# Router logits with the router as stationary operand, and a mixture softmax held on 32 partitions

## What is computed

```python
router_probs = softmax(einsum('bsh,he->bse', x, w_router))
gate_weights = softmax(einsum('bsh,he->bse', x, w_gating) / GATE_TEMP)   # GATE_TEMP = 0.1
g = einsum('bsh,ehf->ebsf', x, w_gate)
u = einsum('bsh,ehf->ebsf', x, w_up)
h = silu(g) * u
expert_out = einsum('ebsf,efh->ebsh', h, w_down)
cw = router_probs * gate_weights
cw = cw / (sum(cw, axis=-1) + 1e-09)
out = einsum('ebsh,bse->bsh', expert_out, cw)
```

## Time and profile before

| | |
|---|---|
| median of 3 runs | 1153.64 us (1153.35 to 1153.64) |
| the profiled execution | 1153.37 us, of which the span from first to last instruction is 1151.4 us |
| granted TensorE clock | 0.999 of full speed |
| busy share of the span | PE 98%, DVE 79%, ACT 61%, POOL 54% |

### The profile page before, as it was taken

How to read it: one execution, slowest core, us unless ns; L and a number is a source line. 1 busy time by engine, 2 the same in 40 slices (tenths; PEclk the granted TensorE clock), 3 DMA queues, 4 the chain that set the end, 5 groups by cost and what they waited for, 6 DMA issues and landing times.

```text
span 1151.4 us, 16819 instructions
## 1 busy us (share of the span) xinstructions
PE 1133.6 (98%) x5102; PEld 928.9 (81%) x5102; DVE 915.2 (79%) x2002; ACT 703.7 (61%) x1370; POOL 622.4 (54%) x480
## 2 busy tenths in 40 slices
PE   8999999999999999999999999999999999999997
PEld 4777888888888888888888888888888888888885
DVE  6798877878888788877878778788887888778765
ACT  6675565655656565575655666566565655756564
POOL 1386564654556455464655556455464655556453
PEclk9999999999999999999999999999999999999999
DMA  4240212102021110212102021111212102020110
GB/s 129 69 128 1 75 37 65 46 20 65 28 74 38 47 43 23 74 37 66 46 12 73 28 75 37 47 38 28 74 38 66 46 6 78 28 72 30 47 51 15
DMA packets 82713, 57.61 MB, mean 50 GB/s; under 512 B 35360, under 2 KB 64192, under 8 KB 82624
## 3 DMA queue, kind: packets, MB, share of 16 engines
q1 hardware_dynamic: 82624, 56.54, 16.8%
HBM read 48.13 MB, written 8.39 MB: 49 GB/s over the span
## 4 chain that ended last, share of the span: by engine, by line
PE 96%; DVE 1%; ACT 1%; DMA 0%; issue 0%; POOL 0%; SPq 0%; POOLq 0%; DVEq 0%; ACTq 0%
PE g L280 10%; PE u L280 10%; PE u L282 10%; PE g L282 10%; PE u L281 10%; PE g L281 10%; PE y L280 10%; PE y L282 10%; PE y L281 10%; PE n_ps L287 2%; PE m_ps L280 1%; PE m_ps L282 1%; PE m_ps L281 1%; PE m_ps L372 1%; PE m_ps L371 1%
## 5 line engine op out<-in xcount | busy, mean ns | idle before, releaser
L1125 POOL TENSOR_TENSOR hid_lo<-hid,hid_hi 128x512 fp32r<-128x512 f32 x255 | 341.3, 1338 | 416.7 <-ACT hid_hi L574 416.5
L568 ACT ACTIVATE gate<-g 128x512 f32<-128x512 f32 x512 | 305.5, 597 | 326.7 <-PE g L282 325.1
L848 DVE TENSOR_TENSOR hid<-gate,u 128x512 f32<-128x512 f32 x512 | 348.5, 683 | 165.1 <-ACT gate L568 133.9
L574 ACT ACTIVATE hid_hi<-hid 128x512 fp32r<-128x512 f32 x512 | 321.1, 627 | 38.5 <-DVE hid L848 38.0
L854 DVE TENSOR_TENSOR hid_lo<-hid,hid_hi 128x512 fp32r<-128x512 f32 x257 | 210.7, 820 | 1.8
L280 PE MATMUL g<-xe_hi,w_hi 128*128 128x512 f32 x512 | 206.4, 403 | 0.1
L280 PE MATMUL u<-xe_hi,w_hi 128*128 128x512 f32 x512 | 199.9, 390 | 1.7 <-DVE hid L848 1.7
L280 PE MATMUL y<-hid_hi,w_hi 128*128 128x512 f32 x512 | 200.1, 391 | 0.3 <-ACT hid_hi L574 0.2
L282 PE MATMUL y<-hid_hi,w_lo 128*128 128x512 f32 x512 | 199.8, 390 | 0.0
L282 PE MATMUL g<-xe_hi,w_lo 128*128 128x512 f32 x512 | 199.7, 390 | 0.0
L281 PE MATMUL g<-xe_lo,w_hi 128*128 128x512 f32 x512 | 199.6, 390 | 0.0
(11 more groups left out here) (205 smaller groups left out, 1131.7 us busy)
## 6 DMA issues: line engine op xcount, KB each, us to landing
cw_b<-cw_scratch SPq DMA_DIRECT2D x128, 256.0 KB, 3.3
x_sb<-x_in SPq DMA_DIRECT2D x16, 256.0 KB, 3.1
out_scratch<-acc_t SPq DMA_DIRECT2D x60, 64.0 KB, 2.3
ffn<-out_scratch SPq DMA_DIRECT2D x15, 256.0 KB, 2.7
x_out<-o_sb SPq DMA_DIRECT2D x15, 256.0 KB, 2.2
stage<-wgate_in SPq DMA_DIRECT2D x8, 256.0 KB, 2.9
stage<-wup_in SPq DMA_DIRECT2D x8, 256.0 KB, 3.4
stage<-wdown_in SPq DMA_DIRECT2D x8, 256.0 KB, 4.2
```

What stands on the lines that cost most here:

```text
L568: nc.scalar.activation(gate[:, k % 2, :], g_ps[k % 2][:], ACT.Silu).then_inc(gate_ready, 1)
L574: nc.scalar.activation(hid_hi[:, k % RING, :], hid[:, k % RING, :], ACT.Copy).then_inc(hi_ready, 1)
L848: nc.vector.tensor_tensor(hid[:, k % RING, :], gate[:, k % 2, :], u_ps[k % 2][:], ALU.mult).then_inc(hid_ready, 1)
L1125: nc.gpsimd.tensor_tensor(hid_lo[:, k % RING, :], hid[:, k % RING, :], hid_hi[:, k % RING, :].bitcast(f32), ALU.subtract).then_inc(lo_pool, 1)
```

## The change

The router becomes the stationary operand. Two products with 512 streamed tokens replace eight short ones: `router` (128 x 32) by `xe_hi`, then the high router (128 x 16) by `xe_lo`. The logits now come out with 32 rows (high and low logits) on the partitions and tokens on the free axis. VectorE turns them with one 32x32-block transposition of [32, 512], after which each of 32 partitions holds 16 tokens of 32 values; all softmax tiles are [32 partitions, 16 tokens, 2, 8]. The weights are written into columns 0 to 7 of blocks of 32 columns of `v_sb`, and a second transposition of [32, 512] gives `cw_t` with one expert per partition, 512 tokens in a row. TensorE's `turn_cw` and ScalarE's copy `cw_t` are gone, and two waits with them. The factor 10 of the second softmax is multiplied into the router once, at the start, instead of into the logits of every chunk. ScalarE's `silus` stands at k = 29 instead of 28.

```diff
-TENSOR_AT = {"turn_cw": 4, "turn_x": 5, ...
+TENSOR_AT = {"turn_x": 5, ...
-SCALAR_AT = {"cw_t": 3, "hi_x": 8, ... "silus": 28}
+SCALAR_AT = {"hi_x": 8, ... "silus": 29}
...
-        lg, e_neg, e_pos = (sb(n, [P, NT, 2, E]) for n in ("lg", "e_neg", "e_pos"))
...
+        lg, e_neg, e_pos = (sb(n, [SMALL, SEQ // SMALL, 2, E]) for n in ("lg", "e_neg", "e_pos"))
...
             def mix_turn_x(c):
                 pe.wait_ge(xn_ready, 2 * c + 1)
-                pe.wait_ge(cw_t_ready, c)
...
-                for j in range(NT):
-                    t, at = slice(j * P, (j + 1) * P), 4 * E * j
-                    nc.tensor.matmul(m_ps[:, at:at + 4 * E], xe_hi[:, par, t], router[:], start=True, stop=False)
-                    last = nc.tensor.matmul(m_ps[:, at:at + 2 * E], xe_lo[:, par, t], router[:, 0, :], start=False, stop=True)
-                last.then_inc(logits_ready, 1)
-
-            def mix_turn_cw(c):
-                pe.wait_ge(cw_ready, c + 1)
-                nc.tensor.transpose(n_ps[:, 0:P], cw_pad[:], ident[:]).then_inc(cw_turned, 1)
+                nc.tensor.matmul(m_ps[0:4 * E, :], router[:].rearrange("p h q -> p (h q)"), xe_hi[:, par, :], start=True, stop=False)
+                nc.tensor.matmul(m_ps[0:2 * E, :], router[:, 0, :], xe_lo[:, par, :], start=False,
+                                 stop=True).then_inc(logits_ready, 1)
...
-            def mix_cw_t(c, first):
-                act.wait_ge(cw_turned, c + 1)
-                if not first:
-                    act.wait_ge(cw_stored, 16 * c)
-                nc.scalar.activation(cw_t[:], n_ps[0:E * NT, 0:P], ACT.Copy).then_inc(cw_t_ready, 1)
...
+            nc.scalar.activation(proj[:, P + D + E:], proj[:, P + D + E:], ACT.Copy, scale=GATE_SHARP).then_inc(gate_scaled, 1)
...
             def mix_softmax_in(c):
-                at = SOFT_LINKS * c
-                pair = "p j r -> p (j r)"
                 dve.wait_ge(logits_ready, c + 1)
-
-                nc.vector.tensor_reduce(out=lg[:].rearrange("p j r e -> p j (r e)"),
-                                        in_=m_ps[:, 0:NT * 4 * E].rearrange("p (j h q) -> p j q h", j=NT, h=2),
-                                        op=ALU.add, axis=AX.X).then_inc(raw_read, 1)
+                nc.vector.transpose(sum_sb[0:SMALL, :], m_ps[0:SMALL, :]).then_inc(raw_read, 1)
                 dve.wait_ge(raw_read, c + 1)
+                parts = sum_sb[0:SMALL, :].rearrange("p (j h q) -> p j h q", h=2, q=2 * E)
+                nc.vector.tensor_tensor(lg[:].rearrange("p j r e -> p j (r e)"), parts[:, :, 0, :], parts[:, :, 1, :],
+                                        ALU.add).then_inc(soft_link, 1)
...
-                nc.vector.tensor_tensor(lg[:], lg[:], sharp[:], ALU.mult).then_inc(lg_ready, 1)
...
-                nc.vector.tensor_tensor(cw_pad[:, 0:E * NT].rearrange("p (e j) -> p j e", j=NT), pr[:],
-                                        wide(den[:], E), ALU.mult).then_inc(cw_ready, 1)
+                wide_rows = v_sb[0:SMALL, :].rearrange("p (j q) -> p j q", q=SMALL)
+                nc.vector.tensor_tensor(wide_rows[:, :, 0:E], pr[:], wide(den[:], E), ALU.mult).then_inc(cw_ready, 1)
+                dve.wait_ge(cw_ready, c + 1)
+                if c > 0:
+                    dve.wait_ge(cw_stored, 16 * c)
+                nc.vector.transpose(cw_t[:], v_sb[0:SMALL, :]).then_inc(cw_t_ready, 1)
```

More of the change, by code:

```diff
@@ L41 @@
 PIECES = WCOLS // F
-TENSOR_AT = {"turn_cw": 4, "turn_x": 5, "bu": 9, "c": 15, "turn_y": 16, "turn_xe": 26,
+TENSOR_AT = {"turn_x": 5, "bu": 9, "c": 15, "turn_y": 16, "turn_xe": 26,
              "logits": 27}
-SCALAR_AT = {"cw_t": 3, "hi_x": 8, "du": 8, "hi_w": 13, "fin_a": 19, "fin_b": 20, "z_a": 18, "z_b": 18,
-             "norm_a": 24, "norm_b": 25, "hi_xe": 26, "silus": 28}
+SCALAR_AT = {"hi_x": 8, "du": 8, "hi_w": 13, "fin_a": 19, "fin_b": 20, "z_a": 18, "z_b": 18,
+             "norm_a": 24, "norm_b": 25, "hi_xe": 26, "silus": 29}
 VECTOR_AT = {"weights": 1, "stats_x": 1, "var_x": 2, "norm_x": 3, "lo_x": 7, "enter": 8, "scan": 9,
@@ L103, in build @@
         pair_mean = sb("pair_mean", [P, NT, 2])
-        sharp = sb("sharp", [P, NT, 2, E])
+        spare = sb("spare", [P, NT, 2, E])
         proj = sb("proj", [P, PROJ])
@@ L134, in build @@
         var_eps, rstd, shift = sb("var_eps", [P, NT]), sb("rstd", [P, NT]), sb("shift", [P, NT])
-        lg, e_neg, e_pos = (sb(n, [P, NT, 2, E]) for n in ("lg", "e_neg", "e_pos"))
[L136 to L139, removed]
+        lg, e_neg, e_pos = (sb(n, [SMALL, SEQ // SMALL, 2, E]) for n in ("lg", "e_neg", "e_pos"))
+        gmax, gsum = sb("gmax", [SMALL, SEQ // SMALL, 2]), sb("gsum", [SMALL, SEQ // SMALL, 2])
+        pr, psum_, den = sb("pr", [SMALL, SEQ // SMALL, E]), sb("psum_", [SMALL, SEQ // SMALL]), sb("den", [SMALL, SEQ // SMALL])
+        cw_t = sb("cw_t", [SMALL, SEQ])
         stats2, mv2 = sb("stats2", [P, NT, 6]), sb("mv2", [P, NT, 2])
@@ L207, in store_cw @@
                 sp.wait_ge(cw_t_ready, c + 1)
-                sp.dma_start(cw_dram[par], cw_t[:]).then_inc(cw_stored, 16)
+                sp.dma_start(cw_dram[par], cw_t[0:E, :]).then_inc(cw_stored, 16)
             def spread_cw(c, par, e, first):
@@ L214, in spread_cw @@
                     sp.wait_ge(part_ready, E * c + e - 3)
-                row = cw_dram[par, e * NT:(e + 1) * NT, :].rearrange("j p -> (j p)")
-                row = row.rearrange("(a t) -> a t", a=1).broadcast_to([P, SEQ])
+                row = cw_dram[par, e:e + 1, :].broadcast_to([P, SEQ])
                 sp.dma_start(cw_b[:, e % 4, :], row).then_inc(cw_spread[e % 4], 16)
@@ L448, in body @@
                         mix_logits(0, 0)
-                    if k == (4 if first else TENSOR_AT["turn_cw"]):
-                        mix_turn_cw(c)
                     if not last:
@@ L619, in body @@
                         mix_silus(0)
-                    if k == (4 if first else SCALAR_AT["cw_t"]):
-                        mix_cw_t(c, first)
                     if not last:
@@ L764, in wide, with mix_peak @@
             def wide(t, n):
-                return t.unsqueeze(2).broadcast_to([P, t.shape[1], n])
+                return t.unsqueeze(2).broadcast_to([SMALL, t.shape[1], n])
             def mix_softmax_in(c):
-                at = SOFT_LINKS * c
-                pair = "p j r -> p (j r)"
                 dve.wait_ge(logits_ready, c + 1)
-                nc.vector.tensor_reduce(out=lg[:].rearrange("p j r e -> p j (r e)"),
-                                        in_=m_ps[:, 0:NT * 4 * E].rearrange("p (j h q) -> p j q h", j=NT, h=2),
-                                        op=ALU.add, axis=AX.X).then_inc(raw_read, 1)
+                nc.vector.transpose(sum_sb[0:SMALL, :], m_ps[0:SMALL, :]).then_inc(raw_read, 1)
                 dve.wait_ge(raw_read, c + 1)
+                parts = sum_sb[0:SMALL, :].rearrange("p (j h q) -> p j h q", h=2, q=2 * E)
+                nc.vector.tensor_tensor(lg[:].rearrange("p j r e -> p j (r e)"), parts[:, :, 0, :], parts[:, :, 1, :],
+                                        ALU.add).then_inc(soft_link, 1)
+            def mix_peak(c):
+                at, pair = SOFT_LINKS * c, "p j r -> p (j r)"
+                dve.wait_ge(soft_link, at + 1)
                 nc.vector.tensor_reduce(out=gmax[:].rearrange(pair), in_=groups(lg), op=ALU.max,
                                         axis=AX.X).then_inc(soft_link, 1)
-                dve.wait_ge(soft_link, at + 1)
+                dve.wait_ge(soft_link, at + 2)
                 nc.vector.tensor_tensor(groups(lg), groups(lg), wide(gmax[:].rearrange(pair), E),
-                                        ALU.subtract).then_inc(soft_link, 1)
-                dve.wait_ge(soft_link, at + 2)
-                nc.vector.tensor_tensor(lg[:], lg[:], sharp[:], ALU.mult).then_inc(lg_ready, 1)
+                                        ALU.subtract).then_inc(lg_ready, 1)
             def mix_exps(c):
@@ L878, in _ @@
             nc.vector.memset(pair_mean[:, :, 1], 1.0 / D)
-            nc.vector.memset(sharp[:, :, 0, :], 1.0)
-            nc.vector.memset(sharp[:, :, 1, :], GATE_SHARP)
-            nc.vector.memset(cw_pad[:], 0.0).then_inc(const_ready, 1)
+            nc.vector.memset(spare[:], 0.0).then_inc(const_ready, 1)
             slope = sum_sb
@@ L1003, in body @@
                         mix_softmax_in(0)
+                        mix_peak(0)
                     if first and k == 1:
```

11 lines of the change are left out of this document (6 added, 5 removed).

## The result

The changed kernel takes 1177.66 us in the median (1176.74 to 1178.55, 4 runs); the kernel before took 1153.49 us beside it (1152.97 to 1153.64, 4 runs). The ratio is 1.021, 95% interval 1.0197 to 1.0223: slower by 24 us, with 1179 predicted. The profiled execution took 1176.74 us with a span of 1174.8 us, 23.4 us more than before.

A forecast was written before the change was run, and what follows sets the result against it. TensorE, busy 98% of the span and 96% of the chain, was taken to bound the kernel. 1153.4 - 8.7 (TensorE's saving) + 30.8 (borders into chunks 1 to 14) + 0.9 (chunk 15) + 2.8 (chunk 0) = 1179 us; range 1146 to 1187.

The forecast's parts named there:

- TensorE's saving: Logits save 0.43 us a chunk and the dropped `turn_cw` 0.11: together 0.54, for 16 chunks 8.7 us.
- The narrow product: Rival: logits with 32 and 16 output rows cost TensorE up to 0.78 us a chunk, 12.5 us, slower; chance 0.06.
- VectorE's durations: Softmax instructions on 32 partitions take time by elements per partition; 2.7 us added before `hid` of unit 2.
- the faster rival: At chunk borders `den` passes ahead of GpSimd, so TensorE never waits there: 1147.5 us; chance 0.18.
- The collision: At chunk borders `den`, two SBUF inputs, comes 0.24 us behind GpSimd's `hid_lo` of unit 31 and is held until 593.25.
- The links behind it: Held instructions of VectorE and GpSimd queue behind `den`; `hid` of unit 2 starts at 599.65, TensorE waits 1.7 us.
- The held `xn`: At borders `xn` is held by GpSimd's `hid_lo` of unit 3, as in chunk 0 (2.10 us); 0.5 us more at `turn_x`.
- The border: Borders into chunks 1 to 14 each lose 1.7 + 0.5 us of TensorE waiting, 30.8 us in all.
- Chunk 0: Softmax in units 0 to 2, where TensorE already waits: 2.8 us more waiting, u of unit 4 at 42.2, `turn_x` at 47.6.

The follow-up runs named there:

- reordered kernel: Changed kernel with the same VectorE instructions, softmax products in the order gsum, pr, den, psum_ instead of pr, gsum, psum_, den: 1147.58 us, ratio 0.9946; again 1146.96 us.
- the version with a quarter of the softmax: Changed kernel with the softmax instructions, not the two transpositions, on 4 of the 16 tokens of each partition: 1145.90 us, ratio 0.9933.
- the version with PSUM inputs: Changed kernel, order kept, with one operand of both `den` and of the last product in PSUM, and one reduction more: 1148.90 us, ratio 0.9956.
- the three places tried: Chunk 0's exps, products and weights in units 1, 1, 2 (reordered kernel, 1146.96 us), 2, 3, 4 (1145.92 us) or 2, 4, 5 (1146.31 us).
- the version with waits of 0.73, 0.96 and 1.02 us: Reordered kernel with chunk 0's exps in unit 2, products in unit 4 and weights in unit 5: 1146.31 us, ratio 0.9934.
- the version that was spread over units 2 to 4: Reordered kernel with chunk 0's exps in unit 2, products in unit 3 and weights in unit 4: 1145.92 us, ratio 0.9933.
- nudged kernel: Reordered kernel with one more short VectorE instruction, a reciprocal of 32 ones, ahead of `den`: 1179.69 us, ratio 1.0227.
- the one before with the reciprocal in unit 30: Kernel before the change, with only a VectorE reciprocal of 32x256 ones added behind the exps of unit 30: 1169.07 us, ratio 1.0133.

## Why the prediction was right

The range, 1146 to 1187 us, held both a faster and a slower kernel, so a time inside it says little. What was tested is the point, 1179, and the chain of instructions behind it, and these hold.

**TensorE's saving** was sized 0.54 us a chunk and measured 0.55 (0.42, and 0.13 by the reordered kernel); a middle chunk of the reordered kernel, where TensorE does not wait at the border, is 0.56 shorter than before. The narrow product costs nothing extra: 593.48, 593.71 and 593.95 are 0.23 and 0.24 apart, and the version with a quarter of the softmax took the 1146 us that follow from no such cost, so that rival is refuted. The Trainium skill, "TensorEngine Tiling (Array Packing)", section "Key Properties", speaks of a drain at a change of tiling mode; for products of 32 and 16 output rows between full ones no drain shows in these starts; whether such a product counts as another mode, no run tells.

**VectorE's durations** follow the elements per partition on 32 partitions as on 128: reciprocal 1.733 us (1.72 predicted), two-input 256 elements 0.41 (0.424), transposition 0.70 (0.705), two-input 128 elements 0.27 (0.30) and 16 elements 0.15 when not held (0.18). That step was the condition of the faster rival, and no duration was off by more than 0.03 us. `psum_` began 3.95 us behind the start of the reciprocal (3.96 laid out).

**The collision.** `den` was predicted 0.24 us behind the start of GpSimd's `hid_lo` and ending with it at once; it starts 0.22 us behind. That so thin a margin came out on the right side rests on the durations of all the instructions ahead of it; the prediction gave the other side 0.18. The links behind it came in the predicted order: addition behind `y_part`, `hid_lo` held, GpSimd's next `hid_lo` first, second `den`, then reciprocal, product, transposition, `stats_x`, `hid`. That the port and not the work makes the wait is shown by the runs with `den` moved, with `den` fed from PSUM, and with 0.33 us put in front of it. The Trainium skill's "SBUF — State Buffer", section "Who interferes with whom", has the exclusive lock, for a VectorE instruction with two SBUF inputs against a GpSimd instruction that reads SBUF. The traces agree, with 0.15 us free and 1.04 to 1.19 us on average held for 16 elements.

The held `xn` was predicted too, at 2.1 us, and is there: 2.10 to 2.12 us in all 15 chunks of the changed kernel, where 14 of the 15 before read as this one:

```profile
599.02 1.11 DVE L692 TENSOR_SCALAR xn<-x_sb,mv,rstd 128x128 f32<-128x128 f32 x4
```

These instructions have one tensor in SBUF as input, so not only two-input instructions are held. In the reordered kernel `xn` is held in the same way (2.12 us in 14 chunks), and TensorE does not wait for it.

**The faster rival** was priced at 1147.5 us for the case in which `den` passes ahead; the reordered kernel, which makes just that case, took 1147.58 and 1146.96 us.

**The sizes.** The border was put at 1.7 + 0.5 = 2.2 us; by the units it is 1.57 + 0.38 and some 0.1 elsewhere, 2.04 in all. `hid` of unit 2 came 11.56 us behind the reciprocal (11.65 laid out); for `turn_x` the 0.5 had been taken over from chunk 0's 0.53 instead of being laid out for a border. The rows give less: `xn` ends at 616.36, and TensorE, which the wait for `hid` had made late itself, starts its last product before `turn_x` at 615.84 and would have been ready some 0.23 behind, at 616.07; `turn_x` starts at 616.42, 0.35 later. 14 x 2.04 = 28.6 us stand against 30.8. Between the two profiled executions 25.8 us were forecast and 23.4 measured, and these 2.2 are nearly all of the difference.

**Chunk 0** was put at 2.8 us of waiting less the 0.54 saved, 2.26 us; the chunk is 2.13 us longer. u of unit 4 came at 41.94 (42.2 predicted) and `turn_x` at 47.18 (47.6). The sum fits in part by luck. At `turn_x` the chunk is 2.06 us behind the kernel before; after that a wait of 0.56 us for `act_lo`, which nobody forecast, and the 0.43 us that the logits of chunk 1 save in unit 27 nearly cancel. The lower clock, below, was not in the reasoning either, and changed nothing at `turn_x`.

## What to carry to other kernels

When work is added to an engine that shares the SBUF port with another, don't ask only whether it fits into the idle time; lay both engines' instructions out on one time axis and look for the first one with two SBUF inputs that changes from just ahead of the other engine's long instruction to just behind it. Here `den` stood 0.09 us ahead in one version and 0.17 and 0.22 us behind in two others, and between the two sides lie 30 us in 1150. Where such a margin is found, move a one-input instruction behind the two-input one, or give the latter an input in PSUM; both turned 2.1% slower into 0.4 to 0.5% faster. The reordered version stands only 0.09 us on the right side, and the version with PSUM inputs does not hang on that margin for its two `den`. One SBUF input is no promise for every operation: beside GpSimd's `hid_lo` a reciprocal took its 1.73 us (changed kernel, 600.26), a reduction 0.28 (PSUM version, 590.06) and a transposition 0.70 (reordered, 593.90), all as when alone, but the four TENSOR_SCALAR of `xn` took 2.1 us instead of 1.1. And where the added work has no idle time to go to, as in chunk 0, it cost time at each of the three places tried.

## What was not expected of the hardware

**The clock behind a wait.** In chunk 0 of the changed kernel TensorE stood from about 39.2 to 41.9 us. Windows of TensorE of that kernel (stretch, length, busy us and count, granted clock, DMA share, GB/s):

```profile
40.00:42.00 2.00, 0.06 (x1) 1.00 0.00 0
42.00:44.00 2.00, 2.00 (x5) 0.50 0.00 0
44.00:46.00 2.00, 2.00 (x7) 0.65 0.07 18
46.00:48.00 2.00, 2.00 (x12) 1.00 0.33 125
```

In the two microseconds behind the wait the granted clock is 0.50, the lower of the two levels (1.2 GHz for 2.4), and from 46 us on it is back at 1.00. The reordered kernel (waits of 2.57 and 2.58 us in its two profiled executions) and the one with PSUM inputs (2.72 us) show the same fall. In the kernel before, where that wait was 1.08 us, and in the version with waits of 0.73, 0.96 and 1.02 us, the clock stayed at 1.00; and so it did around the border wait of 1.41 us in the changed kernel (1.00 in every window from 610 to 618). In the version that was spread over units 2 to 4 it fell behind the wait of 1.84 us. There the windows behind it read:

```profile
44.00:46.00 2.00, 0.32 (x3) 1.00 0.00 0
46.00:48.00 2.00, 2.00 (x10) 0.64 0.00 0
48.00:50.00 2.00, 2.00 (x6) 0.51 0.05 8
```

But the length of the wait alone does not decide. The nudged kernel waited longest at this place, 2.74 us until 42.11, and its clock stayed up:

```profile
42.00:44.00 2.00, 1.89 (x8) 1.00 0.00 0
44.00:46.00 2.00, 1.75 (x8) 1.00 0.06 12
```

What else decides, no run here shows. This kernel also prices the lower clock. With the clock at 1.00 TensorE came to `turn_x` early and waited 0.97 us for `xn`; in the changed kernel the slow products fill that time. `turn_x` starts 14.75 us behind u of unit 0 in the nudged kernel and 14.71 in the changed one, so there the lower clock cost nothing.

**Who goes first when the port comes free.** In the changed kernel GpSimd's `hid_lo`, ready at 608.27 while VectorE's `hid_lo` ran to 608.63, went ahead of VectorE's second `den`, issued 0.29 us after it had become ready. Held instructions thus pass the port to and fro, and one late small instruction is followed by a second. In all three kernels with a late first `den` (changed, nudged, and the one before with the reciprocal in unit 30) the second was held too, and shown 1.18 to 1.19 us long on average; at the borders of the others it never was.
